# A two-layer graph network on one core: 20 instead of 18 groups of edges summed over all node blocks

## What is computed

```python
h = relu(layernorm(x))
msg = where(type == 0, h[src] @ W_data.T + b_data, h[src] @ W_control.T + b_control)
x = x + relu(segment_sum(msg, dst) + h @ W_self.T + b_self)          # layer 0
h = relu(layernorm(x))
g = tanh(p_dst[dst] + p_src[src] + gate_b)                           # p = h @ half of gate_w
e = (g + tanh(yes_no * yes_w + (1 - yes_no) * no_w)) * 0.5 * d[dst] * d[src]
x = x + segment_sum(h[src] * e, dst)                                 # layer 1
```

## Time and profile before

| | us |
|---|---|
| median of 3 runs | 7962.76 |
| lowest and highest run | 7925.66, 7966.09 |
| the profiled execution, its own time | 7983.53 |
| its span, first to last instruction | 7981.7 |
| PE busy in the span | 5574.0 (70%) |
| DVE busy | 4589.0 (57%) |
| POOL busy | 4367.9 (55%) |
| ACT busy | 2870.7 (36%) |

### The profile page before, as it was taken

How to read it: one execution, slowest core, us unless ns; L and a number is a source line. 1 busy time by engine, 2 the same in 40 slices (tenths; PEclk the granted TensorE clock), 3 DMA queues, 4 the chain that set the end, 5 groups by cost and what they waited for, 6 DMA issues and landing times. The chain is left out here.

```text
span 7981.7 us, 117499 instructions
## 1 busy us (share of the span) xinstructions
PE 5574.0 (70%) x28538; PEld 4349.5 (54%) x28538; DVE 4589.0 (57%) x16809; ACT 2870.7 (36%) x9992; POOL 4367.9 (55%) x4284
## 2 busy tenths in 40 slices
PE   5677777777777777777775566777776777777663
PEld 4555555555555555555554545565655565555553
DVE  5755555555555555555444556666666666666662
ACT  4433333333333333333332333333433333333330
POOL 5644444444444444444455366666766666666654
PEclk7577777777777776777776767777878778877875
DMA  6644444444444444444455434444444444444433
GB/s 196 199 139 130 132 135 130 135 135 132 132 136 131 132 136 130 131 131 134 128 165 161 121 85 97 103 100 98 104 98 101 102 103 100 102 101 101 101 90 91
DMA packets 764976, 979.74 MB, mean 123 GB/s; under 512 B 135667, under 2 KB 567063, under 8 KB 763799
## 3 DMA queue, kind: packets, MB, share of 16 engines
q1 hardware_dynamic: 620131, 687.26, 30.0%
q0 software_dynamic: 135168, 281.42, 14.3%
q10 hardware_dynamic: 9012, 3.56, 0.2%
HBM read 911.05 MB, written 60.67 MB: 122 GB/s over the span
## 5 line engine op out<-in xcount | busy, mean ns | idle before, releaser
L564 POOL DMA_INDIRECT G<-t,IDX x4016 | 4077.9, 1015 | 3263.9 <-PE PS L874 1578.9
L699 ACT ACTIVATE OHF<-PS 128x384 bf16<-128x384 f32 x1764 | 853.8, 490 | 2522.5 <-PE PS L892 1313.0
L1031 PE MATMUL PS<-HTB,OWF 128*128 128x129 f32 x3528 | 945.8, 359 | 839.7 <-ACT HTB L801 341.4
L1031 PEld LDWEIGHTS PS<-HTB,OWF 128*128 128x128 f32 x3528 | 813.8, 252 | 1165.9 <-issue 743.1
L782 ACT ACTIVATE ST<-PS,MV 128x1 f32<-128x1 f32 x1764 | 460.1, 261 | 1953.4 <-issue 1670.1
L904 PE MATMUL PS<-CDST,OHF 128*128 128x256 bf16 x5292 | 1115.9, 331 | 7.6 <-issue 5.8
L1040 PE MATMUL PS<-CDST,HTB 128*128 128x256 f32 x2352 | 926.3, 485 | 0.0
L868 PEld LDWEIGHTS PS<-OHF,G 128*128 128x128 f32 x4224 | 814.3, 295 | 154.6 <-issue 108.8
L868 PE MATMUL PS<-OHF,G 128*128 128x32 f32 x4224 | 800.4, 360 | 134.6 <-DVE ACC L1549 52.5
L904 PEld LDWEIGHTS PS<-CDST,OHF 128*128 128x128 bf16 x5292 | 633.2, 120 | 458.6 <-issue 249.0
L1247 DVE TENSOR_SCALAR CDST<-IO,BASE 128x256 bf16<-128x256 int16 x1764 | 503.1, 296 | 590.0 <-PE PS L904 301.2
(11 more groups left out here) (229 smaller groups left out, 8072.4 us busy)
## 6 DMA issues: line engine op xcount, KB each, us to landing
HTB<-t0s SPq DMA_DIRECT2D x442, 384.0 KB
OWF<-t0s SPq DMA_DIRECT2D x440, 384.0 KB
HTB<-t SPq DMA_DIRECT2D x882, 132.0 KB
G<-t,IDX POOLq DMA_INDIRECT x4016
YN<-rows SPq DMA_DIRECT2D x882, 64.0 KB
OHF<-rows SPq DMA_DIRECT2D x882, 64.0 KB
t0s<-HTB SPq DMA_DIRECT2D x25, 384.0 KB
t0s<-OWF SPq DMA_DIRECT2D x24, 384.0 KB
```

The source lines that it names most:

```text
L564: eng.indirect_dma_start(out=G[:, k:k + width], out_offset=None, in_=table, in_offset=bass.IndirectOffsetOnAxis(ap=at, axis=0)).then_inc(s ...
L699: eng.activation(X0[:, k % KX, :, :].rearrange("p n w -> p (n w)"), PS[:, cell_bank(k), 0:384], ACT.Identity).then_inc(q_ev, 1)
L1031: eng.matmul(cell_slot(k), OT1[c % RT][:, col:col + 128], TC1[c % RT][:, k % HB, 0:D + 1], start=True, stop=True).then_inc(d_ga, 1)
```

## The change

`RUNS` is the table of groups. With (20, 62) `DT` becomes 1240, `NG` 20, `SM` 235 and `NCT` 155. `SIZE`, `CELL`, `CELL1`, `TILE` and `ENDS` follow from it. The cells rise from 18 * 98 = 1764 to 20 * 98 = 1960 in each layer, the items fall from 251 to 235 in each.

The tiles to be sorted now take more of the buffer `YN` (`HTE` counts its filled columns), so the third of three one-hot buffers of the gathers in layer 0, `OT0`, moves from `YN` to 256 columns of `CDST` that the ring `CD0` leaves free.

```diff
-RUNS = ((16, 62), (2, 60))
+RUNS = ((20, 62),)
...
         OT0 = [a.bitcast(bf16).rearrange("p (a w) -> p a w", a=2)
-               for a in (W2[:, :], OHF[:, 1792:2048], YN[:, HTE:HTE + 256])]
+               for a in (W2[:, :], OHF[:, 1792:2048], CDST[:, 768:1024])]
         CD0 = CDST[:, 0:KD * DW // 2].bitcast(bf16).rearrange("p (a w) -> p a w", a=KD)
         OHU = [a[:, 0:2 * NB].bitcast(bf16) for a in (BB, MVF)]
-        HTE += 256
         OHBQ = [OHB[:, 0, :], OHB[:, 1, :], YN[:, HTE:HTE + 2 * NB].bitcast(bf16)]
```

## The result

The changed kernel takes 8109.32 us (median of 4 runs, 8084.42 to 8123.19) against 7945.89 us for the kernel before in the same comparison (4 runs, 7925.66 to 7966.09): ratio 1.0202, 95% interval 1.0159 to 1.0245. It is slower by 2.0%, where 1.8% faster was forecast; the time lies inside the range of 7620 to 8160 us. The profiled execution took 8116.17 us, its span is 8113.8 us, 132 us more than the span of before.

A forecast was written before the change was run, and what follows sets the result against it. No engine was full: layer 0 was not bound by POOL and paid for PE's work, while POOL set layer 1's pace. Terms -34 - 6 - 109 + 3 = -146 us from the median 7963 gave 7817 us, range 7620 to 8160.

The forecast's parts named there:

- Layer 0, cells and tiles: Main stage of layer 0: 213 steps of 17.26 us become 199 of 18.3 us, -34 us.
- 18.1 to 18.9 named as the mark: Step time in us expected in the new trace for layer 0 with cells and tiles, at a clock of 0.73 or more.
- In layer 0 POOL does not bound: Layer 0, cells and tiles: POOL is busy only 1456 of 3225 us, 45%, so it does not set the pace.
- the first group's steps: Start of layer 0: 8.18 cells a step took 17.27 us, as long as 7.54 cells, so more cells cost nothing measurable.
- Last stretch of layer 0: Layer 0 with cells but no tiles: 20 steps of 11.2 us become 18 of 12.1 us, -6 us.
- 18 steps with 1.4 cells more each, 0.65 us apiece: Last stretch of layer 0: each added cell costs 0.65 us, giving 218 us in place of 224.
- third rival: Layer 1 falls out of POOL's pace: 14.8 us a step, +252 us in all, 8215 us; chance 0.18.
- Layer 1: Second layer: 250 intervals of 12.70 us become 234 of 13.1 us, -109 us.
- So the cover holds on average: Layer 1: some 5 us of slack cover 1.7 us of added PE work, though a third of steps has 9 cells.
- The example with eight cells in 12.0 us: Layer 1: a fetch cycle with 8 cells took 12.0 us, the usual one 12.1, so PE comes in time for 8.
- the misses that priced the term: Layer 1: 24 plain waits of POOL for PE, 189.3 us together, priced a cycle that misses at 7.9 us.
- The rest: Remaining terms: POOL's nine integer operations ahead of everything grow by at most +3 us; loads, buffer, count items and tables 0.

The follow-up runs named there:

- the run with pairs: Changed kernel with a constant wait count, layer 0's eight fetches issued in four pairs and a wait among layer 1's fetches: 7257.91 us, 0.9145 of the kernel before.

## Why the prediction was wrong

**Layer 0, cells and tiles (-34, measured -33).** Right in size, and partly by luck. Steps took 18.33 us, inside the 18.1 to 18.9 named as the mark, at a clock of 0.79. But "In layer 0 POOL does not bound" is wrong as a reason: POOL was busy 43% of the stage, and yet the run with pairs shows that 4 of these 18 us came from its fetches standing in one run (18.33 to 14.35), in which PE's signals come 3 to 6.5 us late. The prediction took the first group's steps for PE's work with waits to fill and had no term for this. The clock rose with the denser cells, 0.79 against the 0.73 of the earlier trace rows. By the rule of the Trainium skill that activity releases the throttle (TensorE: Matmul & The Clock Gate, What's actually happening) the term would have been -80; the trace agrees in the direction of the clock and not in the size, since at 0.79 PE still ran some 40% of the stage at 1.2 GHz.

**Last stretch of layer 0 (-6, measured +71).** The step that failed is "18 steps with 1.4 cells more each, 0.65 us apiece". Before, 151 / 20 = 7.6 of them fitted POOL's cycle of 11.2 us; with 161 / 18 = 8.9 they do not (161 are ACT's evacuations in the window above), and POOL waits 120.4 us for PE line 873 instead of 16.9. With 19 groups the stretch is back at 12.00 us. This is the third rival's mechanism in a stage in which no rival had placed it.

**Layer 1 (-109, measured +160).** The failed step is "So the cover holds on average". It took the time from 6009.26 to 6014.2 us as 5 us of slack for 1.7 us of added PE work. PE was idle for most of it, but not free. A gather needs the scaling of the cell four before, ACT issues that behind the gate of the cell two before, and that gate needs the signal of its own gather. So PE gets at most two gathers ahead of the last signal that ACT has seen, and a gather made beside POOL's fifth to eighth fetch is taken up 1.7 to 4.4 us late (median) instead of 0.09. The trace of before had it:

```profile
6009.10 0.47 PE L1031 MATMUL PS<-HTB,OWF 128*128 128x129 f32 x2
6009.84 0.39 PE L1031 MATMUL PS<-HTB,OWF 128*128 128x129 f32 x2
6015.06 0.80 PE L1031 MATMUL PS<-HTB,OWF 128*128 128x129 f32 x2 [4.41 <-ACT HTB L801]
```

Two gathers pass, and the third waits until the gate of 6014.19 has answered the first. So an added cell doesn't fill the slack, it goes behind it. What settles this are the runs without fetches (14.27 to 9.88 us a step) and the chips without late signals (10.87 us, no long cycle), both at the same cells. The example with eight cells in 12.0 us was right for itself, but it was one cycle: before had 6 such cycles and none was long, after had 149 and 35 were. And the misses that priced the term were of the other kind, behind a cycle without a pause, so they said nothing of what a cell more does.

**The third rival** (layer 1 falls out of POOL's pace; chance 0.18) is what came. It had a third of the cycles missing at 20 us each; 88 of 226 did, at 16.9 us, so the step was 14.25 us and not 14.8. Its bound, 8% more cycles that miss, was passed by far (from 8% to 39%), and POOL's waits for line 867 came to 701.6 us, above the 400 named as the sign of a wrong forecast. The prediction even had the reason in hand ("only two or three cells can pass while PE's results come late") and gave it too little weight, since in the rows of before the misses were rare.

**The rest (+3, measured -67).** Ahead of the first item 3 us were saved where 3 more were forecast, between the layers 27 and behind the last item 49, while the stretch ahead of the cells cost 11. The 49 us have a plain cause that the prediction did not look for. The last section uses the same five slots of `G` as the items. The wait for its first slot is for the last item that used that slot, `SM - 1 - (SM - 1 - s) % S`. With 251 items that is the very last one, with 235 it is the one four before. So before the change all 104 fetches of the section stand behind the last item, and after it 72. The first chip bears it out: 222 us with 251 items in layer 1, 202 with 243 (two items before) and 173 with 235. It hangs on `SM` modulo 5, and not on the number of groups as such. Between the layers stands the same wait (297 us with 251 items, 292 with 243 on the first chip, 270 with 235).

**What follows for the change.** On chips with late signals 20 groups cost 1.4 to 2.0%, or gained 0.5% on the one where POOL's cycle is 0.2 us shorter; on the others they cost 0.9 to 1.0%. 19 groups were faster by 1.7% on the first chip; with the pairs of fetches the 20 groups are 8.5% faster than the kernel before on the fifth, and on the chips without late signals the pairs give nothing. The pairs were not tried with 18 groups, nor 19 groups with pairs where signals are late, so these 8.5% speak for the pairs and not for 20 groups.

## What to carry to other kernels

Idle time of an engine behind a late signal is no slack: before work is added under a cover, look at what the added work must wait for inside that stretch, and count how many of its links pass there now. One cycle that fits doesn't show that a cover holds; count the share of cycles that miss, by the size of their work, and see whether the misses are of the kind that the added work would make. And where a queue issues many transfers in a run while others need its pauses, try to part the run: on the one chip with late signals where it was tried, the same fetches in pairs brought the kernel 8.5% below the one before, which no count of groups came near.

## What the runs showed of the hardware

- **PE's signals can be late by microseconds while POOL issues indirect DMAs**, and prompt in its pauses and at the start of a run of fetches. In the changed kernel ACT takes a gather of layer 1 up 0.09 us behind its end (median) beside the first three fetches, and 4.05 and 4.43 us behind it beside the fifth and sixth; in the run with pairs, which had the same fetches, the same stage of layer 0 took 14.35 instead of 18.33 us a step. Signals from ACT to PE were not late (0.14 us). Whether DVE's are, and whether POOL's issuing or the transfers that it starts hold the signals, was not told apart. The Trainium skill, Perfetto Trace Analysis, section Per-instruction lifecycle, says that the profiler's end of a matmul is an estimate and that the semaphore goes out only when PSUM has acknowledged the write; it gives no time for that. Here the record of a gather ended at 6040.47 and its reader started at 6045.91.
- **It goes with the chip or its state, not with the program.** The kernel before took 7881, 7956 and 7930 us on three chips and 5868, 5870 and 5877 us on three others; the lag on one of the latter is 0.09 us beside every fetch of layer 1, and the fetches themselves take as long, 1.05 us in layer 1 against 1.03. What sets the two kinds apart wasn't found.
- **PE's clock goes with it.** In layer 0 the granted clock was 0.79 in the changed kernel, 0.91 with the fetches in pairs and 0.98 on a chip without late signals, and the same 15261 matmul records were busy for 2668, 2335 and 2112 us. So a wait for a late signal costs twice, once as a wait and once in the clock. In the cycle shown the clock was 1.00 at the gather of 6043.82 and 0.50 over the item, behind idle times of PE of 2.92 and 1.95 us.
